# Rotated key and query chunks routed through DRAM, and a reordered first unit, in a float32 attention-and-linear kernel

## What is computed

```python
q = (X @ Wq).reshape(b, t, NH, HD).transpose(0, 2, 1, 3)     # NH, NKV, HD = 16, 8, 64
k = (X @ Wk).reshape(b, t, NKV, HD).transpose(0, 2, 1, 3)
v = (X @ Wv).reshape(b, t, NKV, HD).transpose(0, 2, 1, 3)
q = q * cos + _rotate_half(q) * sin
k = k * cos + _rotate_half(k) * sin
att = jnp.einsum('bhqd,bhkd->bhqk', q, jnp.repeat(k, 2, axis=1)) * 256.0 ** -0.5
att = SOFTCAP * jnp.tanh(att / SOFTCAP)                       # 50.0
att = softmax(where(causal, att, -inf))
x = _layernorm(x + (att @ v_repeated).reshape(b, t, NH * HD) @ Wo)
q8, in_scale = per_token_quant_int8(x)
x = _layernorm(x + ((q8 @ weight.T) * in_scale * w_scale + bias).astype(float16))
```

## Time and profile before

| | us |
|---|---|
| median of 3 runs | 1504.92 |
| lowest and highest | 1504.58, 1505.42 |
| the profiled execution | 1501.25 |
| its span in the profile | 1499.3 |

### The profile page before, as it was taken

The page is one execution under the profiler, slowest core; times in us unless marked ns, Lnnn a source line. Parts: engine busy times, 40 slices in busy tenths (PEclk is TensorE's granted clock), DMA queues, the critical chain, the costliest instruction groups (busy, mean ns, idle before and its releaser), DMA issues.

```text
span 1499.3 us, 17504 instructions
## 1 busy us (share of the span) xinstructions
PE 1322.7 (88%) x5824; PEld 963.7 (64%) x5840; DVE 1096.8 (73%) x1367; ACT 849.1 (57%) x952; POOL 380.8 (25%) x448
## 2 busy tenths in 40 slices
PE   6479999978988999897886999999599799999695
PEld 5357777656655777675664777767476477777463
DVE  4369888863677888885486888888258788888485
ACT  4167687752236777764223777687123577779232
POOL 2231111102552111110265112111036312111165
PEclk9789999989988999998998999999799899999896
DMA  7766445474513454547341454446642154343541
GB/s 280 261 205 160 103 129 144 113 211 123 156 50 87 115 139 109 155 96 244 95 133 47 98 137 117 103 144 186 181 123 78 56 137 103 102 110 103 149 109 42
DMA packets 120765, 196.22 MB, mean 131 GB/s; under 512 B 26466, under 2 KB 68964, under 8 KB 116836
## 3 DMA queue, kind: packets, MB, share of 16 engines
q1 hardware_dynamic: 114916, 185.14, 44.2%
q10 hardware_dynamic: 5760, 9.97, 2.0%
HBM read 89.39 MB, written 38.54 MB: 85 GB/s over the span
## 4 chain that ended last, share of the span: by engine, by line
PE 62%; DVE 10%; DMA 9%; SPq 7%; issue 5%; ACT 3%; POOL 3%; ACTq 1%; DVEq 0%; POOLq 0%
PE ps L735 21%; PE ps L655 15%; PE ps L709 14%; PE ps L777 6%; PE ps L677 4%; SPq L427 4%; DMA y_scratch<-sums 3%; DMA rows<-r_scratch 2%; DVE prob_hi L1109 1%; ACT probs L914 1%; DVE stats L1195 1%; DVE probs L1174 1%; DMA qk<-work_r 1%; DMA r_scratch<-inverse 1%; POOL rstd L1332 1%
## 5 line engine op out<-in xcount | busy, mean ns | idle before, releaser
L735 PE MATMUL ps<-prob_hi,v 128*65 128x512 f32 (+3 forms) x1280 | 415.1, 374 | 3.3 <-DVE prob_lo L1113 3.3
L914 ACT ACTIVATE probs<-ps 128x1024 f32<-128x1024 f32 x288 | 293.6, 1020 | 161.9 <-PE ps L709 159.2
L709 PE MATMUL ps<-qk 128*128 128x512 f32 (+1 forms) x1280 | 322.9, 379 | 54.2 <-DMA qk<-work_r 28.4
L1113 DVE TENSOR_TENSOR prob_lo<-probs,prob_hi 128x1024 fp32r<-128x1024 f32 x288 | 360.1, 1250 | 9.9
L1317 POOL TENSOR_SCALAR_AFFINE_SELECT probs<-probs 128x256 f32<-128x256 f32 (+1 forms) x192 | 145.3, 765 | 808.0 <-ACT probs L919 808.0
L919 ACT ACTIVATE probs<-probs 128x1024 f32<-128x1024 f32 x288 | 305.6, 1061 | 8.8
L709 PEld LDWEIGHTS ps<-qk 128*128 128x128 f32 x1280 | 230.1, 193 | 116.9 <-ACT probs L914 27.9
L655 PE MATMUL ps<-xT,w_ring 128*128 128x512 f32 x1152 | 293.5, 399 | 10.0 <-DVE xT L1051 8.0
L1109 DVE CAST prob_hi<-probs 128x1024 fp32r<-128x1024 f32 x288 | 206.3, 716 | 118.5 <-POOL probs L1317 69.6
L655 PEld LDWEIGHTS ps<-xT,w_ring 128*128 128x128 f32 x1152 | 219.6, 193 | 58.3 <-DVE xT L1051 9.3
L735 PE MATMUL ps<-prob_lo,v 128*65 128x512 f32 (+1 forms) x640 | 239.2, 374 | 0.0
(11 more groups left out here) (77 smaller groups left out, 1042.9 us busy)
## 6 DMA issues: line engine op xcount, KB each, us to landing
qk<-work_r SPq DMA_DIRECT2D x256, 128.0 KB, 2.3
qk<-work_r SPq DMA_DIRECT2D x488, 64.0 KB, 2.0
y_scratch<-sums SPq DMA_DIRECT2D x128, 130.0 KB
wo<-wo_scratch SPq DMA_DIRECT2D x8, 2048.0 KB, 7.8
y_raw<-y_scratch SPq DMA_DIRECT2D x64, 256.0 KB, 4.1
w_ring<-w_scratch SPq DMA_DIRECT2D x15, 1024.0 KB, 5.8
x_raw<-X_T SPq DMA_DIRECT2D x16, 512.0 KB, 5.1
x_in<-X SPq DMA_DIRECT2D x32, 256.0 KB, 2.9
```

What stands on the lines that cost most here:

```text
L709: mm = nc.tensor.matmul(scores[:, g % 2, col:col + REP * w].rearrange("p (h q) -> p h q", h=REP), qk[:, n % 2, i, 2 + part, keys], qk[:, n ...
L735: mm = nc.tensor.matmul(sums_ps[:, :, GQ - w:GQ], v[:, kt, v0:v0 + width], p[:, at, col:col + REP * w].rearrange("p (h q) -> p h q", h=REP ...
L914: nc.scalar.activation(probs[:, prob_place(g), :], scores[:, g % 2, :], ACT.Tanh, scale=SCORE_SCALE / SOFTCAP).then_inc(capped, 1)
L1113: nc.vector.tensor_tensor(prob_lo[:, prob_place(g), :], probs[:, prob_place(g), :], prob_hi[:, hi_place(g), :].bitcast(F32), ALU.subtract) ...
```

## The change

1. Each part of a chunk is first sent whole to a DRAM buffer `chunk_scratch` (`send`: one DMA, 128 partitions x 4 KB, 512 KB), and from there taken into `qk` (`take`: for keys 4 DMAs of 32 partitions x 2 x 4 KB, for queries 2 DMAs of 32 partitions x 4 x 2 KB, 256 KB each). `take` waits on SP until its part has landed in DRAM. `qk` is laid out anew for this. `rope_read` waits for sends, not puts. ACT issues no put any more.
2. High and low sends stand at the steps of the old puts; the takes one step later each. Unit 1's takes all stand behind its last send, at s = 15, 16 and 17.
3. First unit: the stages of units 1 to 3 lie in `prob_hi`, behind unit 0's part of `qk`, and in `prob_hi` again; `rope_read(0, ...)` no longer waits for them. PE makes chunks 0 and 1 after six value tiles. SP stores stages 2 and 3 between the sends and takes of unit 0.
4. Wo is loaded after unit 0's takes and split in steps 5 to 8 (ACT) and 6 to 9 (POOL), stored at s = 10.
5. In batches 0 to 2 both parts of Wo are loaded at the end of the batch, behind `load_rows(b, 0)` and `load_rows(b, 1)`; in batch 3 into the place of `xT` at steps 1 and 2 of its last unit. The last two value-weight loads move ahead of the last chunk.

```diff
+    chunk_scratch = nc.dram_tensor("chunk_scratch", [2, 3, 2, P, T], F32, kind="Internal").ap()
...
-        qk = sb("qk", [P, 2, 2, 4, T], F32R)
-        wo = over("wo", "qk", [P, 2, KO, C], F32R, skip=32 * KB)
+        qk = sb("qk", [P, 2, 2 * REP + 4, T], F32R)
+        wo_first = over("wo", "qk", [P, 2, KO, C], F32R, skip=32 * KB)
+        wo_last = over("wo_last", "xT", [P, 2, KO, C], F32R)
...
+        w_stage = over("w_stage", "prob_hi", [P, 3, 2, KC, P], F32R)
+        w_late = over("w_late", "qk", [P, 2, 2, KC, P], F32R, skip=56 * KB)
...
+            def send(m, x, low):
+                sp.wait_ge(rope_lo if low else rope_hi, chunks_upto(m, x))
...
+                sp.dma_start(chunk_scratch[m % 2, x, low], work_r[:, place_of(m, x), 1 - low, :].bitcast(F32)
+                             ).then_inc(chunk_sent[place_of(m, x)][low], 16)
+
+            def take(m, x, low):
+                sp.wait_ge(chunk_sent[place_of(m, x)][low], 16 * ((3 * m + x) // 2 + 1))
+                if m == 1:
+                    sp.wait_ge(wo_stored, 32)
+                if m >= 2:
+                    sp.wait_ge(scored, unit_scored(m - 2))
...
+                for half in range(2):
+                    if x == 0:
+                        src = chunk_scratch[m % 2, 0, low, 64 * half:64 * (half + 1), :].rearrange("(i d) n -> d i n", i=2)
+                        for copy in range(2):
+                            r0 = 64 * copy + 32 * half
+                            sp.dma_start(qk[r0:r0 + 32, m % 2, 2 * REP + 2 * low:2 * REP + 2 * low + 2, :].bitcast(F32), src
+                                         ).then_inc(k_put[m % 2], 16)
+                    else:
+                        src = chunk_scratch[m % 2, x, low, :, half * HT:(half + 1) * HT].rearrange("(h d) n -> d h n", d=32)
+                        r0 = 64 * low + 32 * half
+                        sp.dma_start(qk[r0:r0 + 32, m % 2, 0:2 * REP, (x - 1) * HT:x * HT].bitcast(F32), src
+                                     ).then_inc(q_put[m % 2][x - 1], 16)
...
+            store_stage(0)
+            store_stage(1)
+            send(0, 0, 0)
+            send(0, 0, 1)
+            sp.wait_ge(projected, chunks_upto(0, 0))
+            load_wk(1)
+            take(0, 0, 0)
+            take(0, 0, 1)
+            send(0, 1, 0)
+            send(0, 1, 1)
+            store_stage(2)
+            take(0, 1, 0)
+            take(0, 1, 1)
+            send(0, 2, 0)
+            send(0, 2, 1)
+            store_stage(3)
+            take(0, 2, 0)
+            take(0, 2, 1)
             sp.wait_ge(projected, chunks_upto(0, 2))
             load_wq(1)
+            sp.wait_ge(w_stored[2], 32)
+            sp.dma_start(wo_raw[:, :, :], Wo.rearrange("(k p) n -> p k n", p=P)).then_inc(wo_raw_in, 16)
...
-                        if m == 1 and s == 5:
+                        if m == 1 and s == 10:
                             sp.wait_ge(wo_hi_done, 4)
...
                         if u == UB - 1 and s == 14:
                             load_div(b, 0)
+                            if b + 1 < B:
+                                load_wv(b + 1, 2)
+                                load_wv(b + 1, 3)
                         if at := chunk_at(b, u, s, turns(u, 5, 10, 14)):
-                            put(sp, *at, 0)
-                        if (at := chunk_at(b, u, s, turns(u, 6, 11, 15))) and at != (UB * b + UB, 2):
-                            put(sp, *at, 1)
+                            send(*at, 0)
+                        if at := chunk_at(b, u, s, turns(u, 6, 11, 15)):
+                            send(*at, 1)
+                            if m > 1:
+                                take(*at, 0)
+                        if (at := chunk_at(b, u, s, turns(u, 7, 12, 16))) and m > 1:
+                            take(*at, 1)
+                        if m == 1 and s >= 15:
+                            take(1, s - 15, 0)
+                            take(1, s - 15, 1)
...
-                        if u == UB - 1 and m < U and s in (14, 15):
-                            load_wv(b + 1, s - 12)
-                        if u == UB - 1 and s == 11:
...
+                        if b == B - 1 and u == UB - 1 and s in (1, 2):
+                            load_wo(b, s - 1)
                         if u == UB - 1 and s == 17:
-                            wait_put(sp, last, 1)
-                            wait_put(sp, last, 2)
+                            wait_sent(sp, last, 1)
...
-                for x in range(3):
-                    wait_put(sp, last, x)
+                wait_sent(sp, last, 2)
                 load_rows(b, 0)
...
+                if b + 1 < B:
+                    sp.wait_ge(scored, scores_upto(b, NB - 1))
+                    load_wo(b, 0)
                 put_sums(b, NKV - 1, G - 2)
                 store_inverse(b, 1)
                 load_div(b, 2)
                 load_y(b, 2)
                 put_sums(b, NKV - 1, G - 1)
                 load_rows(b, 1)
+                if b + 1 < B:
+                    load_wo(b, 1)
...
                 project_v(0, t)
                 if t == 1:
                     turn_tables()
-            for x in range(3):
-                project(0, x, 0, 24)
+                if t == 5:
+                    project(0, 0, 0, 24)
+                    project(0, 1, 0, 24)
+            project(0, 2, 0, 24)
...
-                        if b == 0 and u == 0 and s < 4:
-                            split_wo(s)
-                if more:
-                    put(act, UB * b + UB, 2, 1)
+                        if b == 0 and u == 0 and 5 <= s < 9:
+                            split_wo(s - 5)
...
                 if m == 0:
                     dve.wait_ge(tables_kept, 2)
-                    dve.wait_ge(w_stored[UB - 1], 16)
...
-                        if b == 0 and u == 0 and 1 <= s < 5:
-                            split_wo(s - 1)
+                        if b == 0 and u == 0 and 6 <= s < 10:
+                            split_wo(s - 6)
```

More of the change, by code:

```diff
@@ L235, in attention_block @@
         rope_lo = sem("rope_lo")
-        k_put = [[sem(f"k_put{n}{i}") for i in range(2)] for n in range(2)]
-        q_put = [[[sem(f"q_put{n}{f}{i}") for i in range(2)] for f in range(2)] for n in range(2)]
+        chunk_sent = [[sem(f"chunk_sent{n}{low}") for low in range(2)] for n in range(2)]
+        k_put = [sem(f"k_put{n}") for n in range(2)]
+        q_put = [[sem(f"q_put{n}{f}") for f in range(2)] for n in range(2)]
         scored = sem("scored")
@@ L325, in place_of, with wait_sent @@
             return (3 * m + x) % 2
-        def wait_put(eng, m, x):
-            for i in range(2):
-                eng.wait_ge(k_put[m % 2][i] if x == 0 else q_put[m % 2][x - 1][i], puts_upto(m))
+        def wait_sent(eng, m, x):
+            for low in range(2):
+                eng.wait_ge(chunk_sent[place_of(m, x)][low], 16 * ((3 * m + x) // 2 + 1))
         def prob_place(g):
@@ L524, in _, with store_stage @@
                          ).then_inc(wv_stored, 16)
-            for u in range(UB):
+            def store_stage(u):
                 sp.wait_ge(w_hi_done, u + 1)
```

168 lines of the change are left out of this document (79 added, 89 removed).

## The result

| | before | changed |
|---|---|---|
| median us | 1505.17 (4 runs) | 1530.01 (4 runs) |
| ratio, 95% interval | | 1.0148 [1.0108, 1.0188] |
| profiled execution, its span | 1501.25, 1499.3 | 1530.64, 1528.5 |
| MB moved, GB/s | 196.22, 131 | 246.50, 161 |
| PE busy us | 1322.7 | 1341.5 |

The forecast was 1499.1 us, in a range of 1482 to 1514; the time lies outside it, on the slow side. Run again beside the kernel before, the changed kernel gave 1.0147.

The account below looks back on a forecast made before the run. PE was taken to bound the units, with its long waits at seams running through SP. Terms 14.7 - 1.5 - 16.0 - 5 + 9 + 4.6 = 5.8 us gained, from the median of 1504.92 to 1499.1 us, range 1482 to 1514.

Parts of the forecast that it names:

- The take, 1.07 us: Time in the DMA engines for one 256 KB take to 32 partitions, at 245 GB/s; bounds 0.62 and 1.24.
- Unit 1, 16.0: Before unit 1's first score: a loss of 16.0 us, 13.8 wait plus 2.2 slower products; bounds 9.4 and 18.
- Ordinary seams: Later unit seams: second queries' low part arrives within the 9.5 us available, hidden in eight seams, no loss.
- Rival B: Second queries late at every seam because sends land over 1.5 us later than 3.3: 1525 us, chance 0.13.
- The three seams with loads, 5: Unit 2 to 3 of batches 0 to 2, loads between send and take: loss 3 x 1.7 = 5 us.
- the sum 257.6 to 268.6: Seam 2 to 3: send 1.4, high takes 2.1, loads 1.4 + 2.8, low takes 2.1, landing 1.2.
- The start, 14.7 less 1.5: First unit: gain 12.2 from earlier scores plus 2.5 of clock; loss 1.5 from splitting Wo, bounds 0 and 8.4.
- rivals D: First 80 us: stores and takes queue worse than laid out, gain 5 instead of 14.7; 1509 us, chance 0.07.
- C (the splits): Wo's splits on POOL block DVE and PE, loss 8.4 instead of 1.5; 1506 us, chance 0.06.
- Ends of batches, 9: Ends of batches 0 to 2: gain 3 x 3.0 = 9 us, bounds 3 and 15.
- part 4: Ends of batches 0 to 2: value-tile wait goes, PE stops at rows, SP's chain starts earlier, its rest unchanged.
- Last batch, 4.6: Batch 3's output phase: Wo early, sums land in about 2.9 instead of 7.52 us; gain 4.6, bounds 3 and 6.

Follow-up runs that it names:

- x1: Changed kernel with only unit 1's takes moved earlier (keys at s = 12, first queries 13, second queries 15): 1515.39 us, ratio 1.0082 to the kernel before.
- y2: Changed kernel with second queries from unit 1 on straight from SBUF, unit 1's other takes early, input and query-weight loads moved, batch 3's Wo later: 1486.24 us.
- z2: y2 with unit 2's query weights loaded at step 17 of unit 0 instead of step 12: 1484.44 us, ratio 0.9848 to the kernel before.
- x0: The changed kernel run again without edits, beside the variants: 1523.48 us, ratio 1.0147 to the kernel before.
- x3: Changed kernel with the high part's takes issued before the low part is sent: 1538.31 us, ratio 1.0218 to the kernel before.
- x2: Changed kernel with the last input quarter loaded at s = 14 and query weights at s = 17 in batches 0 to 2's third unit: 1507.34 us.
- z1: Changed kernel with SP waiting at the start for unit 0's last takes to land before loading query weights and Wo: 1524.72 us, ratio 1.012.
- x6: Changed kernel with x1 to x4 together, and weight stage 2 stored behind the takes of unit 0's first queries: 1507.64 us, ratio 1.0011.
- z3: z2 with z1's wait at the start and stage 2's store behind the takes of unit 0's first queries: 1483.32 us, ratio 0.9839.
- x4: Changed kernel with the takes of the next batch's second queries moved behind the second rows, ahead of Wo's second part: 1521.05 us, ratio 1.0128.
- y3: y2 with second queries of the first unit of batches 1 to 3 going through DRAM again: 1489.26 us, ratio 0.9882 to the kernel before.
- y4: Kernel before with only the last two value-weight loads of batches 0 to 2 moved ahead of the last chunk: 1501.11 us, ratio 0.9964.
- x7: Kernel before with only the last batch's Wo loaded early, at s = 1 and 2 of its last unit: 1501.40 us, ratio 0.9966.
- y1: Changed kernel with batch 3's two Wo loads at steps 4 and 5 of its last unit instead of 1 and 2: 1524.69 us, ratio 1.0115.

## Why the prediction was wrong, point by point

**The take, 1.07 us.** Right: 1.14 with hardly anything beside the takes.

**Unit 1, 16.0.** The mechanism was right, the size somewhat low. The forecast was a wait of 13.8 and 2.2 behind it; measured were 16.52 and 2.2, together 18.7, just beyond the term's own bound of 18. That the wait alone is near 16.0 is luck. No run takes apart the 2.7 us that the wait was longer. x1, y2 and z2 show that the place of the takes and what is loaded beside them made it: the wait was 16.2 in x0 and 6.8, 6.7 and 3.5 there.

**Ordinary seams, "hidden, with some 1.5 to spare, in eight seams".** Right in seven, which show no wait; the 1.1 to 1.8 of x3 show how little was to spare. Wrong in the eighth. The step that failed is the count: batch 3's seam 2 to 3 was put with the ordinary ones although its units project nothing behind it. The way of 8.4 us was forecast well ("with issue about 8"); the 5.95 us available were never read. +5.2 instead of 0. Rival B, waits in all eight, did not come.

**The three seams with loads, 5.** The mechanism was right and named in the text (loads between send and take); the size was off by more than a factor of three, 18.1. The failed step is the sum 257.6 to 268.6 in which each transfer ran by itself, at its own pace, one behind the other, with one landing of 1.2 at the end. Measured were 5.06 for the send (1.4 in the sum) and 10.37 for the takes. x2 moved the loads and got 17 us back, more than three times the whole term. The wait for `xT` did go, as forecast, but the wait before it is 8.21.

**The start, 14.7 less 1.5.** Two terms were mis-sized. The first is the chain of sends, stores and takes, where the step that failed is the same one as in the seams with loads. First score 70.42 (forecast 67.3), s = 2 at 82.46 (78.5): a send was given 2.8 or 3.3 us and a stage store 4.1, while both went through engines that were full. SP's timeline shows it at chunk 1, whose take could go only when its send had landed, 9.8 us later:

```profile
50.97 0.90 SPq L498 DMA_DIRECT2D chunk_scratch<-work_r  x2
...
60.76 2.00 SPq L519 DMA_DIRECT2D qk<-chunk_scratch  x4
```

The last send took 5.66 and the last takes 9.46. z1 rules out the later loads, and with stage 2's store moved back the first score came at 68.48 (x6) and 66.78 (z3). Of the 2.5 us of clock 1.0 came: the score at s = 2 took 2.07 as before, but the projection behind it 2.63 instead of 3.62. So 9.2 us of 14.7 were gained by s = 3. The second term is the splits of Wo: from there to the arrival at unit 1 3.7 us were lost, for which 1.5 had been counted, most of them in the wait for DVE of 2.53 and the slower projection behind it. Beside POOL's splits two operations of DVE, which take 1.22 and 0.7 us by themselves, took 3.31 and 2.88:

```profile
96.97 3.31 DVE L1168 TENSOR_TENSOR prob_lo<-probs,prob_hi 128x1024 fp32r<-128x1024 f32 x1
100.20 2.88 DVE L1164 CAST prob_hi<-probs 128x1024 fp32r<-128x1024 f32 x1
```

That is 4.3 us ahead of `rope_read(1, 1)`. So rivals D (queueing at the start) and C (the splits) each came in part: 5.5 us short of 14.7 where D had 9.7, and 3.7 lost where C had 8.4.

**Ends of batches, 9.** 2.7 of 9 us came. The wait before the value tiles went largely, as forecast (9.21 to 3.41), and the rows took it back: in batch 0 the waits are 3.41, 4.41 and 3.75, together 11.6, against 9.21 and 4.30, 13.5, and the first rows, which had not been waited for before, now are. The first half of part 4 held in effect: although the last send landed after 5.67 us instead of 3.4,

```profile
342.10 5.67 DMA chunk_scratch<-work_r
```

SP came to the loads of sums 7.1 us behind PE's arrival at the value tiles, against 10.3 before. That is the 3 us that were counted; 3.1 and 4.4 in batches 1 and 2. The failed step is "the rest of the chain follows unchanged". From those loads to the loads of the rows it took 10.1 us instead of the 7.7 from 331.94 to 339.61 in the kernel before (chain of waits of the changed kernel, sums and rows):

```profile
348.66 0.61 SPq L434
...
358.79 0.25 SPq L457
```

Up to the second rows it took 2.9, 3.0 and 3.0 us longer in the three batches, nearly all that had been gained. Four takes now stand right ahead of the loads of sums, but they are not the whole of it: in x4, which moved them, the same stretch still took 9.7 us. Which of the other transfers lengthens it is open. y3 agrees that the detour gives the chain nothing. y4 shows that "the chain is SP's" was too strict: about half of a removed wait did count.

**Last batch, 4.6.** Right: -4.5 in the changed kernel, and 5 us by itself in x7.

**The sum.** The ledger misses the forecast by 35.0 us: seams with loads 13.1, start 7.6, ends of batches 6.3, batch 3's seam 5.2, unit 1 2.7, last batch 0.1. The medians miss it by 30.9, because the profiled execution of the kernel before was 3.7 us below its median. The seams with loads and most of the start, some 18.5 us together, have one cause, shown for the seams by x2 and for the start by the traces and the moved store in x6 and z3: transfers were laid end to end as if each had the DMA engines alone. Batch 3's seam is a lead that was not read. What stays open: how the engines divide between older stores and newer takes at the start (z1's 8.45 us for four takes), and what lengthens the chain at the ends of batches.

## What to carry to other kernels

A transfer whose landing is waited for must be priced with all that was issued ahead of it and has not landed: here the last takes landed in 4 to 5 us, and in 8 to 11 with 1.5 MB ahead of them. A detour through DRAM more than halves the number of DMAs on the queue (22 for 48 per unit) but puts two landings in series, 8.4 us here. It is hidden where a stretch has that much time (keys and first queries) and loses at the last chunk where the stretch is shorter (batch 3's seam) or where loads come between send and takes (the three others); that it gains anything where it is hidden no run shows by itself. Read the available time at every seam separately, above all where a unit has less work than its neighbours, and keep a wait for a landing off a queue that has other chains behind it.

## What the runs showed of the hardware

- Takes of 256 KB from DRAM to 32 partitions ran at 227 to 231 GB/s at a DMA share of 1.04, close to the 245 of puts out of SBUF with 128 KB: source and size together changed the rate by 7%.
- What is issued ahead of a transfer costs it far more than what is issued behind it: with the last input quarter and the query weights taken from ahead of the low takes these landed in 4.13 us (x2), against 8.26 to 10.85 in six executions without that edit. With 4 MB taken from right behind the last takes they landed in 5.14 us (y1) against 5.48 to 6.24; with 3 MB in 8.45 (z1) against 8.53 to 10.46, which is hardly outside what differs between executions. All stood on one queue.
- A landing in DRAM took 2.90 us for 512 KB in a quiet stretch (y1), and 3.8 to 9.8 in stretches with loads, stores or takes beside it.
- Beside a split of Wo on POOL a DVE copy with rounding of 128x1024, 0.69 us without one in the same unit, took 2.88 us, and a subtraction of 1.22 us took 3.31 (changed kernel).
